# One-hot tiles of a graph network: four comparisons with a scalar in place of one broadcast comparison

## The reference

```python
# layer 0: a plain sum over edges, then two dense layers
agg = segment_sum(x[src], dst, N)
h = prelu(bn(((1 + eps) * x + agg) @ W1 + b1)); h = prelu(bn(h @ W2 + b2))
# layer 1: two attention layers
g = h @ W;  e = leaky_relu((g * a_src).sum(-1)[src] + (g * a_dst).sum(-1)[dst])
alpha = softmax of e over the edges of each dst (self loops added)
h = segment_sum(g[src] * alpha, dst, N) + bias
# layer 2: relational attention, 4 relations x 4 heads, then a feed-forward part
# layer 3: a plain sum with degree weights
out = relu(segment_sum((x @ W)[src] * norm, dst, N) + b)
```

## Time and profile before

| what | us |
|---|---|
| median of three timed runs | 9635.6 |
| the three runs | 9623.89, 9655.25, 9635.6 |
| span of the profiled execution, first to last instruction | 8302.2 |
| POOL busy in the span | 5680.5 |
| DVE busy | 5131.6 |
| PE busy | 5101.9 |
| ACT busy | 1947.1 |

### The profile page before, as it was taken

How to read it: one execution, slowest core, us unless ns; L and a number is a source line. 1 busy time by engine, 2 the same in 40 slices (tenths; PEclk the granted TensorE clock), 3 DMA queues, 4 the chain that set the end, 5 groups by cost and what they waited for, 6 DMA issues and landing times. The chain is left out here.

```text
span 8302.2 us, 93571 instructions
## 1 busy us (share of the span) xinstructions
PE 5101.9 (61%) x23571; PEld 3350.7 (40%) x23571; DVE 5131.6 (62%) x19614; ACT 1947.1 (23%) x5001; POOL 5680.5 (68%) x5738
## 2 busy tenths in 40 slices
PE   3444444444434444499899988889878888544433
PEld 3333333344424444344333333333377777433333
DVE  4333364444534555676888888888888888633334
ACT  0000032222222222310223232322354555500001
POOL 7777717777747777311777777777767777577775
PEclk6555565555655565699999999999989999755555
DMA  2111112222222222287787778777767777211111
GB/s 74 52 51 52 51 40 78 78 77 77 70 69 78 78 77 78 61 323 303 252 251 248 248 244 250 244 246 242 222 193 211 210 211 211 61 51 51 52 51 52
DMA packets 434195, 1155.57 MB, mean 139 GB/s; under 512 B 106036, under 2 KB 147476, under 8 KB 420744
## 3 DMA queue, kind: packets, MB, share of 16 engines
q0 software_dynamic: 295984, 849.83, 35.2%
q1 hardware_dynamic: 122892, 275.01, 9.8%
q10 hardware_dynamic: 14796, 24.75, 1.0%
HBM read 1016.65 MB, written 132.52 MB: 138 GB/s over the span
## 5 line engine op out<-in xcount | busy, mean ns | idle before, releaser
L953 POOL DMA_INDIRECT gat_ring<-gat_table,psrc_idx x1664 | 1616.9, 972 | 776.7 <-issue 495.5
L589 DVE TENSOR_TENSOR acc<-acc,bank 128x129 f32 (+1 forms) x1664 | 480.7, 289 | 1233.1 <-PE bank L552 1188.5
L1936 POOL DMA_INDIRECT pair<-right_table,idx_r_idx x782 | 787.7, 1007 | 362.1 <-issue 213.4
L2096 POOL DMA_INDIRECT msg<-left_table,pidx_idx x832 | 805.8, 969 | 276.4 <-issue 238.0
L1936 POOL DMA_INDIRECT acc<-left_table,idx_l_idx x782 | 797.1, 1019 | 238.4 <-issue 209.0
L521 POOL DMA_INDIRECT gcn_sum_ring<-gcn_table,src_idx x782 | 769.1, 983 | 274.4 <-issue 237.7
L521 POOL DMA_INDIRECT gin_sum_ring<-in_x,src_idx x782 | 768.9, 983 | 250.7 <-issue 237.4
L1975 PE MATMUL bank<-pair,ident 128*128 128x512 f32 x1564 | 835.6, 617 | 64.1 <-DMA pair<-right_table,idx_r_idx 64.1
L1998 ACT ACTIVATE positive<-acc 128x512 f32<-128x512 f32 x782 | 492.4, 630 | 1577.1 <-DVE acc L2026 1576.9
L552 PE MATMUL bank<-gcn_sum_ring,gcn_sum_hot 128*128 x1664 | 418.2, 431 | 618.0 <-DMA gcn_sum_ring<-gcn_table,src_idx 585.0
L1017 PE MATMUL bank<-gat_ring,gat_hot 128*128 128x130 f32 x3328 | 715.4, 390 | 121.3 <-DVE gat_hot L1137 119.7
(11 more groups left out here) (553 smaller groups left out, 9393.5 us busy)
## 6 DMA issues: line engine op xcount, KB each, us to landing
gat_place<-local_rows SPq DMA_DIRECT2D x128, 416.0 KB, 3.7
left_table<-rel_out SPq DMA_DIRECT2D x49, 1032.0 KB, 4.8
right_table<-rel_out SPq DMA_DIRECT2D x49, 1032.0 KB, 3.9
feat<-attr_rows SPq DMA_DIRECT2D x194, 256.0 KB, 5.7
gat_ring<-gat_table,psrc_idx POOLq DMA_INDIRECT x1664
types<-type_rows SPq DMA_DIRECT2D x98, 256.0 KB, 4.5
msg<-left_table,pidx_idx POOLq DMA_INDIRECT x832
gin_sum_ring<-in_x,src_idx POOLq DMA_INDIRECT x782, 2.5
```

Of the source, the lines that this page charges most:

```text
L953: e.indirect_dma_start(ring[:, at:at + TROW], None, table[:, :], bass.IndirectOffsetOnAxis(ap=ed["psrc"][:, i:i + 1], axis=0)).then_inc(*g ...
L1936: e.indirect_dma_start(to[j % NG][:, n * LROW:(n + 1) * LROW], None, tab[:, :], bass.IndirectOffsetOnAxis(ap=idx[:, i:i + 1], axis=0)).the ...
L2096: e.indirect_dma_start(rows[j % NG][:, n * LROW:(n + 1) * LROW], None, left[:, :], bass.IndirectOffsetOnAxis(ap=ed["pidx"][:, i:i + 1], ax ...
```

## The change

Two places make the one-hot tiles in another way. Before, one `tensor_tensor` compares 512 columns: `node_iota` repeated four times against four columns of `local`, each spread over 128 columns. After, each of the four tiles has a `tensor_scalar` of 128 columns, which compares `node_iota` with one column of `local`, one scalar for each partition. In the attention layers the last chunk keeps the old form.

```diff
@@ aggregate_rows
                 def make(b, made):
-                    e.tensor_tensor(
-                        hot_of(b)[:, :].rearrange("p (t n) -> p t n", n=P),
-                        c["node_iota"][:, :].unsqueeze(1).to_broadcast([P, Q, P]),
-                        over(ed["local"][:, b * Q:(b + 1) * Q], P), ALU.is_equal).then_inc(*made.up())
+                    for n in range(Q):
+                        m = e.tensor_scalar(hot_of(b)[:, n * P:(n + 1) * P], c["node_iota"][:, :],
+                                            ed["local"][:, b * Q + n:b * Q + n + 1], None, ALU.is_equal)
+                    m.then_inc(*made.up())
@@ gat_edges, sums(cn)
-                            e.tensor_tensor(
-                                hot[i % NH][:, :].rearrange("p (t n) -> p t n", n=P),
-                                c["node_iota"][:, :].unsqueeze(1).to_broadcast([P, HQ, P]),
-                                over(ed["local"][:, i * HQ:(i + 1) * HQ], P), ALU.is_equal).then_inc(*hot_made.up())
+                            if cn < CHUNKS - 1:
+                                for n in range(HQ):
+                                    m = e.tensor_scalar(hot[i % NH][:, n * P:(n + 1) * P], c["node_iota"][:, :],
+                                                        ed["local"][:, i * HQ + n:i * HQ + n + 1], None, ALU.is_equal)
+                            else:
+                                m = e.tensor_tensor(
+                                    hot[i % NH][:, :].rearrange("p (t n) -> p t n", n=P),
+                                    c["node_iota"][:, :].unsqueeze(1).to_broadcast([P, HQ, P]),
+                                    over(ed["local"][:, i * HQ:(i + 1) * HQ], P), ALU.is_equal)
+                            m.then_inc(*hot_made.up())
```

## The result

| | median, us | runs, us |
|---|---|---|
| kernel before | 9649.5 | 9623.89 to 9676.5, 15 runs |
| kernel after | 9670.0 | 9647.38 to 9702.07, 15 runs |
| forecast | 9564 | range 9538 to 9608 |

The ratio is 1.0025, 95% interval [1.0016, 1.0034]: the change costs about 24 us by the ratio (20 us by the medians), just inside the 0.3% that the prediction called no change. The forecast had the wrong sign.

A forecast was written before the change was run, and what follows sets the result against it. GpSimd's indirect gathers were taken to pace the kernel. Gathers no longer held gain 83.1 us, less 8 for new holds and 3.6 for tails: 71.5 us off 9635.6, giving 9564 us, range 9538 to 9608.

The forecast's parts named there:

- every plain-sum and attention stage is paced by them: In the plain sums and attention layers, GpSimd's indirect gathers, one per 128 edges, set the pace; GpSimd busy 5680.5 us.
- over unscaled: The 71.5 us gain on the profiled span was taken unchanged to the timed runs: 9635.6 to 9564 us.
- Rival 2: Whole kernel: no change, long gathers stay or the 1333 us outside the span hide the gain; 9639 us, chance 0.12.
- The cover of VectorE's time: Plain sums and attention: nearly all of 161 us more VectorE work hides under waits, 23 us a chunk in attention.
- Gathers no longer held: Plain sums and attention: gathers starting inside the 512-wide comparison are no longer held, a gain of 83.1 us.
- The first two terms: First and last plain sums: gains from gathers no longer held, 27.9 us and 25.9 us.
- rival 3: Attention: other VectorE instructions hold gathers and give back 29.3 us; gain only 45 us, 9591 us, chance 0.15.
- Gathers held by the new form: Plain sums and attention: the four tensor_scalar still hold some gathers, a cost of 8 us, between 0 and 17.
- Rival 1: Changed batches: four tensor_scalar act as one block holding gathers, 250 us; 170 us slower, 9806 us, chance 0.06.
- The tails: End of each plain sum, gathers over: nine batches go from 1.77 to 1.97 us, costing 1.8 us, twice, 3.6 us.

The follow-up runs named there:

- e0: The kernel before, with no edit, run again for a trace of the long time: 9554.2 us, ratio 0.9997, trace span 9568.7 us.
- e1: Against the kernel before, only the two plain sums get four tensor_scalar comparisons; attention layers keep the broadcast one: 9576.4 us, ratio 1.0013.
- the fourth session's change: The whole change run again against the kernel before (8316.6 us), at the short time: 8262.2 us, ratio 0.9932.
- e4_change_again: The whole change run again against the kernel before (8321.2 us), in the second session: 8267.8 us, ratio 0.9935.

## Why the prediction was wrong

**The step that failed** is the first of the prediction, "every plain-sum and attention stage is paced by them", together with the one that took the gain "over unscaled" to the timed runs. Both were read from an execution of 8302.2 us, and the timed runs take 1333 us more. The prediction said that what fills those "is not in the trace" and kept them apart from the stages. They are inside the stages: in e0 the first sum's gathers run to 1149.0 us in place of 1033.1, the attention layers' from 1350.4 to 3874.3 us in place of 1205.6 to 3426.7. The three changed stages hold 519 of the 1266.5 us between the two traces (116, 303 and 100), layer 2 another 680. In these stages GpSimd stops for room in its ring, so gathers do not set the pace, and what they gain comes back as idle time. Rival 2 had the place (the gap hides the gain) and 9639 us, and came closest, but put the cost at the 3.6 us of the tails.

**The cover of VectorE's time** was 23 us of waiting a chunk. At the long time there is none in 30 of 32 chunks (78.5 us in 2), in the kernel before as in the changed one (86.0 us in 2). VectorE has other idle time there, for late products (1223.9 and 685.4 us), and a one-hot batch comes only behind it. How much of the 161 us more of VectorE work lies open by this is not shown: e1 has half of that work and lost 12 us or none.

**Gathers no longer held.** Right as a mechanism at either time: 983 ns to 949 and 954, as forecast (945 to 960). Attention has 967 at the long time, above the forecast 955 to 965, and 962 at the short time, within it. At the short time the gain can be sized. The groups by line of the fourth session's change:

```profile
L953 POOL DMA_INDIRECT gat_ring<-gat_table,psrc_idx x1664 | 1601.3, 962 | 784.8 <-issue 495.8 <-POOLq L830 278.4 <-PE bank L1017 10.7
...
L521 POOL DMA_INDIRECT gcn_sum_ring<-gcn_table,src_idx x782 | 749.4, 958 | 275.9 <-issue 236.8 <-POOLq L2261 37.9 <-PE bank L552 1.2
L521 POOL DMA_INDIRECT gin_sum_ring<-in_x,src_idx x782 | 744.4, 952 | 250.5 <-issue 236.2 <-ACTq L512 12.5 <-PE bank L552 1.8
```

Against the earlier trace rows that is 24.5, 19.7 and 15.6 us less, 60 us in all, where the prediction had 83.1 - 8 = 75. The first two terms are near 27.9 and 25.9. Attention was put at 29.3 and gave 15.6: starts inside the new L1139 carry 9.7 us over 945 ns there, and those inside L1053, which spreads the slots, 6.1 us in place of 4.0, a small part of what rival 3 expected.

**Gathers held by the new form** was put at 8 us, with 17 as its upper end. At the short time it is 17 us: 3.0 in the first sum, 4.5 in the last (over its own 952 ns), 9.7 in attention. Rival 1, the run of four as one block with 250 us, falls: a start inside the run costs 17 ns on average in the first sum (961 against 944) and 52 in attention (996 against 944), where the rival needed 150. A run of four is four short holds with gaps between them, the longest 83 ns in the first sum. The Trainium skill, "SBUF — State Buffer", section "Who interferes with whom", says that an instruction in a 2-port mode, which `tensor_scalar` can enter, holds the shared pair for its whole length and blocks the other side fully. The traces agree that a gather is blocked fully, but not for the whole length of the row: at 128 columns the hold is over 0.15 us after the start of an instruction whose row is 0.27 to 0.30 us long, and the measurement decides.

**The tails.** From the start of the last gather to that of the last addition the first sum took 26.9 us before and 29.8 in the fourth session's change, 30.4 in the second's, 2.9 and 3.5 us more; the last sum took 27.2 before and 28.9 and 29.2, 1.7 and 2.0 more. For each 1.8 was forecast. Six of the eight periods of the first sum's tail are 1.95 or 1.96 us, near the forecast 1.97, and two are 2.2 to 2.4, which makes most of the rest. Two starts in `e4_change_again`:

```profile
1021.53 0.87 DVE L569 TENSOR_SCALAR gin_sum_hot<-node_iota,e_local 128x128 f32<-128x128 f32 x4
...
1023.48 0.86 DVE L569 TENSOR_SCALAR gin_sum_hot<-node_iota,e_local 128x128 f32<-128x128 f32 x4
```

So the forecast of -71.5 us was one for the short time, where -54 and -57 were measured. At the long time the same change gave +24 and +14. That the short-time figures lie near the forecast bears out its terms for the gathers and the tails; it does not make the forecast right for the time that was measured.

**What stays open.** What holds the completions at the long time: it is there with no change to the kernel and on one chip at one time and not at another, and those traces lack most of the records that would show it. All 11 traces of the long time hold 45,000 to 47,000 records of semaphore updates, all 9 of the short time 122,000 to 123,000. So the recording differs together with the time, and no run tells whether it takes part in the holds. How the 54 us of gathers turn into a loss that varies from 14 to 66 or 76 us between sessions is not settled either; in the two sessions where the loss was largest the kernel before was the quickest of the long ones (9561.6 and 9572.2 us), and there it sits in the attention layers. That VectorE's time costs at the long time rests on the order in the table alone: its theory missed the size in six runs at that time, and the lead of two batches, which should have helped by it, did nothing. Layer 2, which is not changed, takes 4474 to 4543 us in such traces, so a single trace cannot settle it. Of the versions that ran at both times, only one of 512 beat the kernel before at both, and its tiles are not the reference's.

## What to carry to other kernels

Set a profile's span beside the timed runs before anything is read from it; if they are 16% apart, the waits of that profile are not those of the time that is measured, and cover ("this engine waits 23 us here anyway") has to be shown again in a trace of the right length. Relief for the engine that seems to set the pace is worth nothing where that engine stops for room that the others make. Weigh a trade of one engine's time for another's under both conditions. A version that leaves part of the result out can size such a trade, but it is no replacement: two instructions of 256 columns took all of the relief at the short time, with less of VectorE's time than before, with half of their one-hot tiles wrong.

## What the runs showed of the hardware

- Width holds an indirect gather more than the operation does. A gather that is held goes on at a fixed point after the instruction's start: 0.15, 0.22 and 0.35 us for a `tensor_scalar` of 128, 256 and 512 columns, 0.16 and 0.56 us for a `tensor_tensor` of 128 and 512, about 0.5 and 1 ns more for each column more. A `tensor_tensor` of 512 columns lengthened gathers by 0.27 and 0.41 us in the earlier trace rows, while four of 128 leave the first sum's mean at 952 ns, near the 949 of four `tensor_scalar` of 128.
- A `tensor_scalar` of 512 columns takes 0.40 us from start to start against 0.60 for the broadcast `tensor_tensor`, but a gather that starts inside it takes 1061 ns on average in place of 944 (1023 in a second run), beside 1213 for the `tensor_tensor`; beside 256 columns 959, beside 128 961.
- Cutting it costs: 0.40 us a batch in one instruction, 0.53 in two, 0.78 in four. As an estimate from these three, each cut adds 0.13 us, and a column takes about 0.5 ns. A `tensor_tensor` takes 0.60 us in one and 0.81 in four, so each cut adds 0.07 us there and a column about 1 ns, and the gap of 0.2 us at 512 columns is gone when both are cut into four.
- The same program on the same chip (the first and the second session) took 9561.6 and 8321.2 us. The mean granted clock of TensorE, as a share of full speed, is 0.722 to 0.73 in the first session's runs of the kernel before and 0.733 to 0.74 in the second's, 1.4% apart in the median where the times are 15% apart; the waits for a release that the trace does not show (1265.0 us ahead of L589 in the trace of 9568.7 us, none in that of 8302.2 us) are where the traces differ most.
